# Attention: window maxima by halves of the heads, another order of all engines, context query rows copied within SBUF

## The reference

```python
# x: [8, 512, 256], ctx: [8, 64, 256]; 16 heads of 16
h  = layernorm(x)
q, k, v = split(h @ w_qkv.T)                      # window attention
# a query sees the keys (q-128, q] from key 16 on, and the first 16 keys up to itself
x1 = x + softmax(mask(q @ k.T / 4)) @ v @ w_out.T
h2 = layernorm(x1)                                # context attention over 64 keys, with a mask
x2 = x1 + (softmax(mask((h2 @ Wq + bq) @ (ctx @ Wk + bk).T / 4)) @ (ctx @ Wv + bv)) @ Wo + bo
# then attention over the sequences of a position (8 of them), 4 heads, layernorm,
# and a mixture of 8 experts (one per token, 256 -> 1024 -> 256), layernorm
```

## Time and profile before

| | us |
|---|---|
| median of 3 runs | 1405.59 (1402.73 to 1405.93) |
| profiled execution, whole time | 1400.48 |
| its span | 1398.8 |
| granted TensorE clock, mean | 0.924 |
| busy in the span: TensorE, VectorE, ScalarE, GpSimd | 1174.2, 755.4, 512.0, 449.7 |
| attention program ends at about | 815 |

### The profile page before, as it was taken

One profiled execution on the slowest core, in us unless ns is written; L12 is line 12 of the kernel. 1 busy time (PEld: TensorE's weight loads), 2 busy tenths in 40 slices (PEclk: granted clock), 3 DMA queues, 4 the chain that ended last, 5 costly groups with the idle time before them and its releaser, 6 DMA issues. The chain is left out here.

```text
span 1398.8 us, 27398 instructions
## 1 busy us (share of the span) xinstructions
PE 1174.2 (84%) x8686; PEld 785.2 (56%) x8687; DVE 755.4 (54%) x2163; ACT 512.0 (37%) x1081; POOL 449.7 (32%) x668
## 2 busy tenths in 40 slices
PE   3788798998989989989786547999986499999997
PEld 1344444454445454544443224666665399999996
DVE  2626448366473674645732224665656356556654
ACT  4062351533624426244162104454442233333331
POOL 2052241333422314223132001443433244444443
PEclk8789799999998999999999779999998699999998
DMA  6426436164352642536501234255433511111110
GB/s 172 106 66 139 113 92 147 41 145 106 85 127 58 147 113 59 126 67 140 111 3 36 57 111 130 93 173 142 120 128 128 174 49 51 53 53 56 48 56 8
DMA packets 94082, 133.86 MB, mean 96 GB/s; under 512 B 23821, under 2 KB 75536, under 8 KB 89297
## 3 DMA queue, kind: packets, MB, share of 16 engines
q1 hardware_dynamic: 88944, 119.28, 34.3%
q0 software_dynamic: 4512, 12.92, 2.4%
q10 hardware_dynamic: 576, 1.06, 0.2%
HBM read 91.42 MB, written 42.18 MB: 96 GB/s over the span
## 5 line engine op out<-in xcount | busy, mean ns | idle before, releaser
L846 ACT ACTIVATE probs<-ps_b 128x512 f32<-128x512 f32 (+2 forms) x352 | 175.6, 538 | 139.4 <-PE ps_b L1063 101.2
L552 POOL TENSOR_SCALAR_AFFINE_SELECT probs<-probs 128x512 f32<-128x512 f32 x128 | 81.4, 636 | 238.6 <-ACT probs L846 234.0
L2387 PE MATMUL ps_c<-keep_w,e_hT 128*128 x624 | 141.0, 379 | 0.0
L2387 PEld LDWEIGHTS ps_c<-keep_w,e_hT 128*128 128x128 f32 x624 | 115.7, 190 | 14.1
L1029 PE MATMUL ps_a<-k_rows,q_rows 96*128 96x256 bf16 (+1 forms) x512 | 92.4, 280 | 28.0 <-DVE top L651 25.0
L651 DVE CUSTOM_DVE_ANT_0 ps_a<-ps_a,mask_qk 128x256 f32<-128x256 f32 x256 | 100.3, 456 | 10.6 <-PE ps_a L1029 9.4
L2343 ACT ACTIVATE e_w_now<-keep_w 128x1024 f32 x78 | 78.3, 1050 | 33.4 <-PEq L1589 21.0
L1029 PEld LDWEIGHTS ps_a<-k_rows,q_rows 96*128 96x128 bf16 x512 | 42.1, 101 | 73.8 <-DVE top L651 39.2
L622 DVE SCALAR_TENSOR_TENSOR rest<-ps_d,parts 128x512 f32<-128x512 f32 x32 | 22.0, 688 | 111.1 <-ACT parts L830 111.1
L1063 PE MATMUL ps_b<-q_rows,k_rows 98*128 98x256 bf16 (+1 forms) x512 | 79.8, 268 | 0.9
L644 DVE TENSOR_REDUCE top<-ps_a 128x2 f32<-128x512 f32 (+1 forms) x96 | 62.8, 686 | 29.3 <-PE ps_a L1029 27.9
(11 more groups left out here) (225 smaller groups left out, 2382.9 us busy)
## 6 DMA issues: line engine op xcount, KB each, us to landing
qk_parts<-parts SPq DMA_DIRECT2D x96, 128.0 KB
e_row<-sorted_rows SPq DMA_DIRECT2D x39, 258.0 KB, 2.6
keep_w<-in_e_w SPq DMA_DIRECT2D x16, 512.0 KB, 4.3
keep_w<-in_e_w SPq DMA_DIRECT2D x8, 1024.0 KB, 8.6
q_rows<-qk_parts SPq DMA_DIRECT2D x16, 384.0 KB, 5.0
k_rows<-qk_parts SPq DMA_DIRECT2D x16, 384.0 KB, 7.6
ctx_q_parts<-q_parts SPq DMA_DIRECT2D x48, 128.0 KB
q_rows<-ctx_q_parts SPq DMA_DIRECT2D x16, 384.0 KB, 5.8
```

The source lines that it names most:

```text
L552: nc.gpsimd.affine_select(own, own, [[0, TILES], [1, P]], ALU.is_ge, keep_zero, base=0, channel_multiplier=-1).then_inc(probs_cut.sem, 1)
L846: nc.scalar.activation(probs[:, user % 2, lo:lo + width], ps_exp[:, f % 2, 0:width], ACT.Exp).then_inc(exp_done.sem, 1)
L2387: mm = nc.tensor.matmul(ps_out[:, s, 0:D], hT[:, s, f, :], w2[:, bass.ds(e * KF * D + f * D, D)], start=(f == 0), stop=(f == KF - 1))
```

## The change

- The maxima of a sequence are taken in two halves of heads, 15 fills each (`HALF_ORDER`): the half 0 (heads 0 to 7, groups 0 and 1) of sequence n+1 during the later part of iteration n (`early_scores`, `early_maxima`), the half 1 (heads 8 to 15) of sequence n in the first part of iteration n (`late_scores`, `late_maxima`). Each half has its own shift, transposes and two DMAs (`window_shift`, shiftA and shiftB, `stack_shift`).
- The order of all engines is new: an iteration begins with the shifted fills of group 0; features and keys of the next sequence are done early in it, context attention after group 2.
- The context query weights are scaled and permuted once so that a partition of their product is (feature of a head, head). Then each part can be copied by DMA from `q2_parts` into 16 rows of `q2_rows` at a time: twelve copies of 128 KB (`stack_context_queries`) in place of six stores and six loads.
- Values of the prefix keys are no longer computed by matmuls but copied by four DMAs from `v_ones` (`copy_prefix`). Values of sequence n+1 are computed at the end of iteration n.
- The context mask is made by GpSimd instead of VectorE. Shift tiles are 32 columns wide instead of 128.

GpSimd's new order: cuts of group 0, mask, layernorm rstd, cuts of group 1 with the low parts of queries and keys of the next sequence's tile 0 and those of the context queries between them, bias onto x1, low parts of tile 1, cuts of groups 2 and 3, low part of the context keys, rstd of sequence n+2. ScalarE's: exponentials of group 0 around copies of heads and features; group 1 around high and middle parts and the context features; sums 0 and 1; shift copies; exponentials of group 2, of the eight context pairs, and of group 3 around context keys; sums 3; values of the next sequence.

The diff, cut to its core; of the functions `iteration` of SP, VectorE and TensorE (in this order) the new text stands, without the lines taken out.

```diff
-FRONT_FILLS = ["xT0", "xT1", "q0", "k0", "q1", "k1"]
-FILLS = ["s3", "oT0", "oT1", "out0", "out1", "v0", "xT2_0", "xT2_1", "q2_0", "q2_1", "v1", "shiftT", "vg", "ctxT",
-         "k2", "shiftT2", "xT0", "xT1", "q0", "k0", "q1", "s0", "k1", "v2", "out2_0", "out2_1", "s1", "s2"]
+FRONT_FILLS = ["xT0", "xT1", "q0", "k0", "q1", "k1", "shiftA", "v0", "v1"]
+FILLS = ["s3", "oT0", "oT1", "xT0", "xT1", "out0", "out1", "q0", "k0", "xT2_0", "xT2_1", "q2_0", "q2_1", "s0",
+         "q1", "shiftB", "k1", "s1", "shiftT2", "s2", "shiftA", "ctxT", "k2", "v2", "out2_0", "out2_1", "v0", "v1"]
-CROSS_MAX, WINDOW_MAX = 2 * TILES, 30
-EARLY_MAX = 4
-EARLY_BEFORE_S2 = min(EARLY_MAX, 1)
-SCORE_MAX = CROSS_MAX + WINDOW_MAX
-BEFORE_S3, BEFORE_HEADS, BEFORE_OUT0, BEFORE_OUT1, BEFORE_V0, BEFORE_V1, BEFORE_Q0, BEFORE_Q1 = 6, 8, 10, 12, 14, 16, 18, 20
+PROJECTIONS = ("q0", "k0", "q1", "k1")
+HALF = HEADS // 2
+MASKED_BY_PE = (0, 1)
+PREFIX_FILL = (TILES, 0)
+HALF_ORDER = [(0, 0), (0, 1), (1, 0), (1, 1), (1, 2), (1, 3), (2, 0), (2, 1), (2, 2), (2, 3), PREFIX_FILL, (3, 0), (3, 1), (3, 2), (3, 3)]
+CROSS_MAX, HALF_MAX = 2 * TILES, len(HALF_ORDER)
+BEFORE_CROSS = 0
+BEFORE_CONTEXT = GROUPS - 1
+SCORE_MAX = CROSS_MAX + 2 * HALF_MAX
+MAX_AHEAD = 3 * HALF_MAX - SCORE_MAX
-WINDOW_ORDER = [(c, j) for half in range(2) for c in range(TILES) for j in range(8) if j // (2 if c == 0 else 4) == half]
-HALF_FILLS = len(WINDOW_ORDER) // 2
-WINDOW_ORDER[-2:-2] = [(2, 8), (3, 8)]
-PROJECTIONS = ("q0", "k0", "q1", "k1")
-MASKED_BY_PE = (0, 1)
...
+    def stack_context_queries(n, tile, parts_):
+        heads = slice(8 * tile, 8 * tile + 8)
+        for block_, part, count in STACKS:
+            if part in parts_:
+                sig = (q2_hi, q2_mid, q2_lo)[part]
+                for rows in range(block_ * HD, (block_ + count) * HD, HD):
+                    sp.dma_start(q2_rows[rows:rows + HD, heads, :],
+                                 q2_parts[:, part, tile, :]).then_inc(q2_loaded[tile].sem, 16)
...
+    def stack_shift(n, h):
+        sp.wait_ge(shiftT_ready.sem, shiftT_ready.next(n, 1) if h == 0 else shiftT_ready.count(n, 2))
+        for part in range(2):
+            sp.dma_start(q_rows[SPLIT_ROWS + part:SPLIT_ROWS + part + 1, top_half(h), :],
+                         shiftT[h][part * HALF:(part + 1) * HALF, :]).then_inc(shift_stacked[h].sem, 16)
+    def copy_prefix(n):
+        sp.wait_ge(v_ready.sem, v_ready.count(n, KD))
+        for j in range(GROUP):
+            sp.dma_start(v_prefix[32 * j:32 * j + 32, j:HEADS:GROUP, 0:HD], v_ones[0:32, 0, j:HEADS:GROUP, 0:HD]
+                         ).then_inc(vprefix_loaded.sem, 16)
...
     def iteration(n, last=False, ahead=True):
         first = isinstance(n, int) and n == 0
+        copy_prefix(n)
         if not first:
             sp.wait_ge(ctxT_ready.sem, ctxT_ready.count(n, 0))
         for rep in range(2):
             sp.dma_start(ctx_in[rep * CTX:(rep + 1) * CTX, :], t["ctx"][n]).then_inc(ctx_loaded.sem, 16)
+        if ahead:
             sp.wait_ge(ln_done.sem, ln_done.next(n, TILES))
             load_x(n + 2)
+        if first:
+            sp.wait_ge(consts_set.sem, 10)
+        else:
             sp.wait_ge(x1_ready.sem, x1_ready.count(n, 2))
         sp.dma_start(x_res[:, :, :], tiles_of(t["x"][n])).then_inc(xres_loaded.sem, 16)
+        if not last:
+            store_front(n, 0)
+        if not first:
+            stack_context_queries(n, 0, range(3))
+            stack_context_queries(n, 1, range(1))
+        if not last:
+            stack_front(n, 0)
+        if not first:
+            stack_context_queries(n, 1, range(1, 3))
+        stack_shift(n, 1)
+        if not first:
+            stack_shift2(n)
+        if not last:
+            store_front(n, 1)
         if not first:
             sp.wait_ge(mask_ready.sem, mask_ready.count(n, 1))
         sp.dma_start(mask_in[:, :, :], tiles_of(t["mask"][n])).then_inc(mask_loaded.sem, 16)
         if not last:
+            stack_shift(n, 0)
+            stack_front(n, 1)
+        split_context_keys(n)
         if not first:
             store_x2(n)
...
         store_front(-1, tile)
         stack_front(-1, tile)
+    sp.wait_ge(ln_done.sem, TILES)
+    load_x(1)
+    stack_shift(-1, 0)
...
+    def window_shift(n, h):
+        place = early_max(n, HALF_MAX) if h == 0 else late_max(n, HALF_MAX)
+        own = n + 1 if h == 0 else n
+        dve.wait_ge(max_free.sem, max_free.count(n, place))
+        nc.vector.tensor_tensor(top[:, 2:4, top_half(h)], top[:, 2:4, top_half(h)], top_prefix[:, :, top_half(h)],
+                                ALU.max).then_inc(top_joined.sem, 1)
+        dve.wait_ge(top_joined.sem, top_joined.count(own, h + 1))
+        shift_parts(own, top[:, :, top_half(h)], shift[h], HALF, shift_hi, h + 1, shift_ready)
...
     def iteration(n, window=True, cross=True, last=False, ahead=True):
+        front = window and not last
         if cross:
             normalise_heads(n, GROUPS - 1)
             dve.wait_ge(xres_loaded.sem, xres_loaded.count(n, 0))
             dve.wait_ge(x2_stored.sem, x2_stored.count(n, 0))
+            residual(n, ("out0",), x_res, x1, x1_ready)
+        if window:
+            late_maxima(n, (0,))
+        if window:
+            late_maxima(n, (1,))
+        if cross:
+            residual(n, ("out1",), x_res, x1, x1_ready)
             dve.wait_ge(x1_ready.sem, x1_ready.count(n, 2))
             layernorm_statistics(nc, dve, x1, stats2, moments2, passed, ln2_stats, ln2_moments, n)
         if window:
+            late_maxima(n, (2,))
+        if front:
+            split_rest(n, (0,))
+        if window:
+            late_maxima(n, (3,))
         if cross:
             layernorm_apply(nc, dve, x1, xn2, moments2, rstd2, ln2_rstd, ln2_done, n)
+        if window:
+            late_maxima(n, (4,))
+        if front:
+            split_rest(n, (1,))
+        if window:
+            late_maxima(n, (5, 6, 7))
         if cross:
             context_query_rest(n, 0)
         if window:
+            late_maxima(n, (8, 9))
         if cross:
             context_query_rest(n, 1)
         if window:
+            late_maxima(n, range(10, 14))
+            normalise_heads(n, 0)
+            late_maxima(n, range(14, HALF_MAX))
+            window_shift(n, 1)
+        if front:
+            split_rest(n, (2,))
+        if cross:
+            context_maxima(n, range(TILES))
+        if front:
+            split_rest(n, (3,))
+        if cross:
+            context_maxima(n, range(TILES, TILES + 2))
+        if window:
+            normalise_heads(n, 1)
+        if cross:
+            context_maxima(n, range(TILES + 2, CROSS_MAX))
+            context_shift(n)
+        if front:
+            early_maxima(n, range(13))
+        if window:
+            normalise_heads(n, 2)
+        if front:
+            early_maxima(n, range(13, HALF_MAX))
+            window_shift(n, 0)
+        if cross:
+            normalise_cross(n, 0)
+        if ahead:
+            ln_statistics(n + 2)
+        if cross:
+            normalise_cross(n, 1)
         if window:
             context_key_rest(n)
             context_values(n)
         if cross:
             dve.wait_ge(x1b_ready.sem, x1b_ready.count(n, 1))
             residual(n, ("out2_0", "out2_1"), x1, x1, x2_ready)
+        if ahead:
+            ln_apply(n + 2)
     dve.sem_inc(max_free.sem, 2)
...
     split_rest(-1, range(4))
     dve.wait_ge(consts_set.sem, 7)
-    early_maxima(-1, range(EARLY_MAX))
+    ln_statistics(1)
+    early_maxima(-1, range(HALF_MAX))
+    window_shift(-1, 0)
+    ln_apply(1)
     iteration(0, cross=False)
     with dve.Fori(1, B - 2) as n:
         iteration(n)
...
     def iteration(n, window=True, cross=True, last=False):
+        front = window and not last
+        late = iter(range(HALF_MAX if window else 0))
+        early = iter(range(HALF_MAX if front else 0))
+        def late_scores(count):
+            for f in islice(late, count):
+                window_scores(n, 1, f)
+        def early_scores(count):
+            for f in islice(early, count):
+                window_scores(n, 0, f)
+        if window:
+            window_shifted(n, 0, 0)
         if cross:
             sums_transposes(n, GROUPS - 1)
+        if window:
+            window_shifted(n, 0, 1)
         if cross:
             heads_transposes(n)
+        if front:
+            for k in range(KD):
+                features(n, k)
+        if window:
+            window_shifted(n, 0, 2)
         if cross:
             output(n, "out0", oT, w_out, oT_ready)
+        if window:
+            window_shifted(n, 0, 3)
+        late_scores(2)
         if cross:
             output(n, "out1", oT, w_out, oT_ready)
+        if window:
+            window_shifted(n, 0, GROUP)
+        late_scores(2)
+        if front:
+            queries_or_keys(n, 0)
+        if window:
+            window_shifted(n, 1, 0)
+        late_scores(1)
         if front:
             queries_or_keys(n, 1)
```

(119 more changed lines are left out.)

602 lines of the change are left out of this document (238 added, 364 removed).

## The result

The changed kernel takes 1421.39 us (median of 4 runs, 1416.06 to 1424.02) where the kernel before took 1404.41 on the same chip: a ratio of 1.0116, 95% interval 1.0084 to 1.0149. It is slower; 1361 was predicted. Its profiled execution has a span of 1414.4 us, 15.6 more than before.

| stretch | before | predicted | after |
|---|---|---|---|
| to the first residual addition | 125.15 | 131.5 | 145.18 |
| first full iteration | 98.2 | 87 | 96.5 |
| five steady iterations | 447.1 (89.4 each) | 424 (84.8) | 448.7 (89.7) |
| last iteration with window work, to its second addition (751.60; after 764.37) | 81.1 | 70 | 74.0 |
| context-only stretch, to the last residual addition | 61.8 | 55.8 | 64.4 |

What follows compares the result with a forecast made beforehand. TensorE was taken as nearest to a bound, with about 19 of 89.4 us waits and lower clock. Savings -6.4 + 11 + 23 + 11 + 6 = 45 us gave a median of 1361; main range 1338 to 1376, 8 in 10 1330 to 1392.

Steps and rivals of the forecast that it cites:

- The order of the engines: Steady iteration: 69.4 us TensorE work, 12.7 waits and 2.7 switching give 84.8 against 89.4; 23 saved over five.
- switching: TensorE, steady iteration: some 35 more switches between short pieces at 0.05 to 0.1 us each, 2.7 us.
- The second context tile: Steady iteration, before context scores: copies taking 4.5 us land at t = 38.5, wanted at 37; 1.5 us wait.
- Prologue: Before and in iteration 0: later sequence 1 load, first residual at 131.5 instead of 125.15; 6.4 us lost.
- First full iteration: First full iteration: 87 us against 98.2, with TensorE fed evenly; 11 us saved, bounds 3 and 13.
- Last iteration with window work: Last window iteration: half the maxima, 52.8 us TensorE work, 17 waits; 70 against 81.1, 11 saved.
- Context-only stretch: Last stretch, only context work: copies replace stores and loads; 6 us saved (4 to 7).
- Row loads exposed: Rival, 0.12: half 0's row loads take 17 us, context scores and early fills wait; 92.5 us an iteration, about 1415.
- The waits come back: Rival, 0.18: in-order queues let one late operation hold others; 88 us steady, 1385 in all (1376 to 1401).
- TensorE-bound: Rival, 0.12: engines running ahead swallow short waits, 7 us instead of 15.4; 77 us an iteration, 1319 in all.

Runs made afterwards that it cites:

- experiment 2: Changed kernel with all six copies of the second context tile issued on SP ahead of the next sequence's rows; 1397.1 us, ratio 0.9956.
- 5: Changed kernel's order, but context query rows go through DRAM by six stores and six loads as in the kernel before; 1455.81 us, ratio 1.0383.
- 3: Changed kernel with each of the twelve copies going to 128 partitions instead of 16, same bytes, rows not the reference's; 1375.93 us, ratio 0.9807.
- experiment 12: Changed kernel with early sequence 1 load, second tile's copies ahead, and copies to 128 partitions, rows not the reference's; 1343.33 us, ratio 0.9572.
- Experiment 1: Changed kernel with the load of sequence 1 issued ahead of the prologue's row loads; 1402.21 us, ratio 0.9993.
- experiment 9: Kernel of 7, with sequence 0's values computed ahead of the first maxima instead of just before iteration 0; 1377.66 us, ratio 0.9834.
- 10: Kernel of experiment 9, with context shift transposes and two shifted heads of group 2 ahead of the first early fill; 1373.61 us, ratio 0.9818.
- 7: Changed kernel with both edits on SP: sequence 1's load ahead of the first rows, second tile's copies ahead of the next sequence's rows; 1377.39 us, ratio 0.9809.
- 11: Kernel of 7, with context shift transposes and two shifted heads of group 2 ahead of the first early fill; 1377.86 us, ratio 0.9818.

## Why the prediction was wrong

- **The order of the engines (right in kind, its total partly by luck).** A walk of 12.7 us of waits, 2.7 of switching and 69.4 of work, without the 1.5 for the second tile, gives 83.3; the iteration without its 7.9 us wait is 81.8. The parts do not fit as well: beside that wait TensorE stands idle 6.0 us where the walk had 11.2, and it is busy 75.7 us (clock 0.96) where I had 72.1 of work and switching. Two errors nearly cancel. VectorE's load is even, and the waits for maxima fell to 0.8 us, as in the list of experiment 2.
- **The second context tile (the step that failed).** I priced "a copy of 128 KB between 2.5 us and 6.9", took 4.5 and bounded the wait by 4. That is the latency of one transfer, and it was the queue's length that counted: nine copies and six loads of rows are ahead. My text had the last copies there at t = 38.5, before the rows ahead of them in the same queue (by t = 40), and I did not see it. They hold the DMA engines from 526 to 551, and the last copies land after 12.7 us, not 4.5. The wait is 7.9 us, not 1.5: 6.4 too little in each steady iteration. Of the 60 us missed, 24.7 lie in the five steady iterations and 9.5 in the first full one, less than six times 6.4, because of the two errors above; the prologue has 13.7, the last window iteration 4.0 and the context-only stretch 8.6. The rate was in my text, 15 us an iteration for the twelve, and did not enter the sum. Experiments 2 and 5 show that the place in the queue costs it, 3 and 12 that the narrow copies do.
- **Prologue.** Forecast: VectorE at 50, iteration 0 at 66.5, first residual at 131.5. Measured: 55.8, 75.0, 145.18. The load took 9.3 us instead of 4 to 6, and the values of sequence 0, between the shift's transposes and iteration 0 at low clock, were left out of the path. From there to the first residual addition it is 70.2 us, not 65; TensorE is busy 59.5 of them at a clock of 0.90, and no run takes this part alone. Experiment 1 takes 18 of the 20 us back: I had priced the late load at 12.7 us of delay, and did not ask what it cost to issue it earlier.
- **First full iteration.** 87 forecast, 96.5 measured: waits of 3.7 and 7.2 us for the copied rows of the two tiles, and a clock of 0.91 where I had TensorE fed evenly. With both edits it is 89.7.
- **Last iteration with window work.** 70 forecast, 74.0 measured. Here it is the work: TensorE is busy 61.2 us where I had 52.8, and idle 12.8 where I had 17; the second tile's wait is 1.4 us.
- **Context-only stretch.** 6 us saved were forecast, 2.6 were lost. Up to the first context fill 3.8 us were saved (21.8 us after the second addition instead of 25.6), though it came 9.1 us behind the first issue. From there on 6.4 were lost (42.6 instead of 36.2): the second tile waits 2.3 us, and TensorE is busy 29.2 us at a clock of 0.59 where it was 23.9 at 0.77. The sum had no term for the clock.
- **The rivals.** "Row loads exposed" had the sign, the cause (copies into 16 partitions share the DMA engines) and the price, 7 to 8 us an iteration; but which rows waited depends on SP's order: as written it is the second tile's, and the next sequence's only once the copies go first. I gave it 0.12 by the mean DMA share of 0.46, a mean over an iteration, where the transfers that matter fall into 25 us. "The waits come back" is refuted: they did not. "TensorE-bound" had the short waits nearly right (7 us, measured 6.0) but not the work: 70 us against 75.7 busy, and even with no wait for a DMA left (experiment 12) the iteration is 81.2, not 77.

Open stays how much of the clock's level after a wait or a move becomes time, as in experiment 9: it is only seen here. A way to lay the same rows at the rate of experiment 12 was not found either.

## What to carry to other kernels

Price a transfer by what stands ahead of it in the DMA engines: add up the bytes of the whole burst, each at the rate measured for its form (here 128 GB/s with the engines full for copies into 16 partitions), and compare with the time until the last of it is wanted; the latency of one transfer and a mean share tell neither. When an order is changed so that a consumer comes earlier, put its transfer first and look who is now last: here two moved lines on SP turned 1% slower into 1.9% faster (1377.39 us, ratio 0.9809), and each wait removed afterwards named the next one. When two errors in a forecast can cancel, compare its parts with the profile, and not only its total.

## What the runs showed of the hardware

- Twelve copies within SBUF, each into 16 partitions, fill the DMA engines at 128 to 129 GB/s, on one queue or on two (15.1 and 14.8 us from first issue to use for 1.57 MB). To 128 partitions the same bytes move at 182 GB/s with the engines about half busy (share 0.54), and a copy lands in 2.1 us instead of 5.8 (medians).
- TensorE's granted clock was 1.00 before it sat idle for 7.9 us and 0.62 over the 5 us after. From 55 to 75 us it was 0.72 and 0.86 in the two kernels where 5.5 us of dense fp32 matmuls had been moved away from just ahead of iteration 0 (experiments 9 and 10), and 0.96 and 0.98 in the two that have them there and are otherwise the same (7 and 11).
